# First attention of a two-block kernel: turned queries and keys kept by heads, each head's scores in four products of 32 queries

## The reference

```python
q = (layernorm(x) @ Wq).reshape(B, Sq, H, D)          # 16 batches, 128 queries, H = 16, D = 128
k = (ctx @ Wk).reshape(B, Skv, H, D)                  # 128 keys
v = (ctx @ Wv).reshape(B, Skv, H, D)
q, k = rmsnorm(q, gq), rmsnorm(k, gk)
attn = softmax(einsum('bqhd,bkhd->bhqk', q, k) / sqrt(D))
x = x + einsum('bhqk,bkhd->bqhd', attn, v).reshape(B, Sq, H * D) @ Wo
```

## Time and profile before

| | |
|---|---|
| median of 3 runs | 2107.34 us (2105.96 to 2109.98) |
| the profiled execution | 2104.1 us, its span 2102.3 us |
| mean granted TensorE clock | 0.985 |
| TensorE busy | 2030.6 us, 97% of the span |
| VectorE, ScalarE, GpSimd busy | 1341.8, 753.5, 580.9 us |
| score products (L415) busy | 142.7 us |
| send and bring | 64 of each, 512 KB, median 5.0 and 4.1 us to landing |

### The profile page before, as it was taken

One profiled execution on the slowest core, in us unless ns is written; L12 is line 12 of the kernel. 1 busy time (PEld: TensorE's weight loads), 2 busy tenths in 40 slices (PEclk: granted clock), 3 DMA queues, 4 the chain that ended last, 5 costly groups with the idle time before them and its releaser, 6 DMA issues.

```text
span 2102.3 us, 33004 instructions
## 1 busy us (share of the span) xinstructions
PE 2030.6 (97%) x12144; PEld 1665.1 (79%) x12144; DVE 1341.8 (64%) x2451; ACT 753.5 (36%) x2307; POOL 580.9 (28%) x713
## 2 busy tenths in 40 slices
PE   6999999989999889999999999999999999999999
PEld 5788888778888778888888867777778888888887
DVE  6665555565555456434335368888867888887886
ACT  4444444554444344311112145545443312222211
POOL 3322222452222232531012133333310123232321
PEclk9999999999999999999999999999999999999999
DMA  5522222333333343312002210000112256555554
GB/s 211 185 97 90 100 97 90 130 114 108 110 107 128 120 130 106 101 40 81 33 27 73 84 62 19 20 17 20 46 48 73 87 185 200 189 177 190 192 166 160
DMA packets 119503, 221.48 MB, mean 105 GB/s; under 512 B 10608, under 2 KB 65904, under 8 KB 119408
## 3 DMA queue, kind: packets, MB, share of 16 engines
q1 hardware_dynamic: 95696, 133.22, 18.8%
q0 software_dynamic: 23712, 87.04, 12.7%
HBM read 169.90 MB, written 50.33 MB: 105 GB/s over the span
## 4 chain that ended last, share of the span: by engine, by line
PE 59%; DMA 17%; DVE 11%; ACT 8%; issue 4%; POOL 1%; SPq 0%; DVEq 0%; ACTq 0%; POOLq 0%
PE bank L48 23%; PE four_banks L48 23%; DMA turned<-blocks 9%; DMA qkT<-turned 6%; PE four_banks L415 4%; ACT junk_k L514 3%; PE bank L1467 3%; ACT prob L525 3%; DVE blocks L658 2%; DVE blocks L648 2%; DVE k_sb L655 2%; PE four_banks L1538 2%; PE bank L1564 1%; PE bank L1576 1%; DVE l_rotB L1943 1%
## 5 line engine op out<-in xcount | busy, mean ns | idle before, releaser
L2363 POOL DMA_INDIRECT m_ring<-in_table,m_row x128 | 127.7, 997 | 369.6 <-DVE l_x_all L2476 263.4
L48 PE MATMUL four_banks<-l_yT_hi,m_hi 128*128 128x512 f32 x512 | 199.4, 389 | 0.0
L48 PE MATMUL four_banks<-l_yT_lo,m_hi 128*128 128x512 f32 x512 | 199.2, 389 | 0.0
L525 ACT ACTIVATE prob<-four_banks,mx,rms 128x128 f32<-128x128 f32 x256 | 113.9, 454 | 207.6 <-DVE mx L665 207.6
L415 PE MATMUL four_banks<-qkT 128*128 128x128 f32 x512 | 142.7, 436 | 31.5 <-DMA qkT<-turned 27.2
L415 PEld LDWEIGHTS four_banks<-qkT 128*128 128x128 f32 x512 | 126.6, 332 | 54.2 <-DMA qkT<-turned 53.7
L310 POOL TENSOR_TENSOR rms<-ssq,constants 128x4 f32<-128x4 f32 x128 | 26.7, 208 | 497.9 <-ACT junk_k L514 312.9
L1133 DVE TENSOR_SCALAR f_relu<-bank,f_b 128x512 f32<-128x512 f32 x64 | 48.0, 750 | 166.3 <-ACT f_h_hi L1076 166.2
L1076 ACT ACTIVATE f_h_hi<-bank,f_b 128x512 fp32r<-128x512 f32 x64 | 44.1, 690 | 256.9 <-PE bank L48 256.9
L313 POOL TENSOR_TENSOR rms<-rms,constants 128x4 f32<-128x4 f32 x128 | 130.7, 1021 | 10.0
L662 DVE TENSOR_REDUCE mx<-four_banks 128x4 f32<-128x512 f32 x64 | 44.2, 691 | 122.0 <-PE four_banks L415 122.0
(11 more groups left out here) (288 smaller groups left out, 5673.3 us busy)
## 6 DMA issues: line engine op xcount, KB each, us to landing
turned<-blocks SPq DMA_DIRECT2D x64, 512.0 KB, 5.0
qkT<-turned SPq DMA_DIRECT2D x64, 512.0 KB, 4.1
f_stage<-in_w POOLq DMA_DIRECT2D x14, 512.0 KB, 4.6
f_x_in<-x SPq DMA_DIRECT2D x18, 256.0 KB, 3.3
ctx_in<-in_ctxT SPq DMA_DIRECT2D x32, 128.0 KB, 3.5
x_in<-in_x SPq DMA_DIRECT2D x16, 256.0 KB, 2.6
x<-xres SPq DMA_DIRECT2D x16, 256.0 KB, 2.0
x<-l_x_all SPq DMA_DIRECT2D x16, 256.0 KB, 2.0
```

The source lines that it names most:

```text
L48: mm = pe.matmul(out, st, mv, start=first and n == 0, stop=last and n == len(terms) - 1)
L525: a = act.activation(prob[g][:, j, :], bank[(1, 3)[g]][:, j * P:(j + 1) * P], ACT.Exp, bias=mx[g][:, 1, j:j + 1], scale=rms[g][:, 0, j:j + 1],
L2363: pool.indirect_dma_start(ring[slot][:], None, table, bass.IndirectOffsetOnAxis(ap=row[:, tile_of(g), k:k + 1], axis=0)).then_inc(S[f"got{ ...
```

## The change

`blocks` and `qkT` are kept by slot: 32 elements of one head lie side by side, so the transposes write and the products read runs of 32 floats. A head's scores are no longer one product with 128 columns of queries held, but four with 32 each, every one into its own 32-partition strip of the bank; the keys are streamed as 4 x 32. SP issues both sends before both brings, each with a semaphore of its own. VectorE turns the queries of half 0 before it copies the probabilities of half 1. The loads, low parts and high parts of the ReLU network's weights are issued later in steps 25 to 28 (SP's behind the brings, POOL's behind the means of the queries, ScalarE's behind the squares). Two semaphores of x's pieces become one.

```diff
--- before.py
+++ after.py
@@ -115,10 +115,9 @@
     ctxp = parts("ctx", [P, KC, P])
 
 
-
     k_sb = sb("k_sb", [P, G * D], F32)
-    blocks = [sb(f"blocks{g}", [P, 4, 32, 2 * G], F32) for g in range(2)]
-    qkT = [sb(f"qkT{g}", [P, 4, 32, 2 * G], F32) for g in range(2)]
+    blocks = [sb(f"blocks{g}", [P, 4, 2 * G, 32], F32) for g in range(2)]
+    qkT = [sb(f"qkT{g}", [P, 4, 2 * G, 32], F32) for g in range(2)]
     v_sb = [sb(f"v_sb{g}", [P, G * D], F32) for g in range(2)]
     junk = {n: sb("junk_" + n, [P, slots, D], mybir.dt.bfloat16) for n, slots in (("q", G), ("k", 2 * G))}
     prob = [sb(f"prob{g}", [P, G, P], F32) for g in range(2)]
@@ -137,10 +136,10 @@
     mx = [sb(f"mx{g}", [P, 2, G], F32) for g in range(2)]
     den = [sb(f"den{g}", [P, 2, G], F32) for g in range(2)]
 
-    names = """ident_loaded x_loaded ctx_loaded xres_loaded0 xres_loaded1 xres_loaded2 xres_loaded3 xres_loaded4 xres_loaded5
-        g_loaded stats_ready ln_eps ln_ready xn_ready xT_turned xT_hi xT_lo ctx_hi ctx_split set stored eps_added qk_stored
+    names = """ident_loaded x_loaded ctx_loaded xres_loaded0 xres_loaded1 xres_loaded2 xres_loaded3 xres_loaded4
+        g_loaded stats_ready ln_eps ln_ready xn_ready xT_turned xT_hi xT_lo ctx_hi ctx_split set stored eps_added
         s_turn y_begun y_ready y_added wq0_staged wv_staged wk_staged wq1_staged wo0_staged wo1_staged""".split()
-    names += [f"{n}{g}" for g in range(2) for n in """q_made k_made v_made q_blocks k_blocks qk_loaded v_copied q_squared
+    names += [f"{n}{g}" for g in range(2) for n in """q_made k_made v_made q_blocks k_blocks qk_stored qk_loaded v_copied q_squared
         k_squared q_rms k_rms scored bias_ready exped normed p_turned pT_copied mixed oT_hi oT_lo""".split()]
     PIECES = ("wq0", "wq1", "wk0", "wk1", "wv0", "wv1", "wo0", "wo1")
     names += [f"{n}_{what}" for n in PIECES for what in ("hi", "cut")]
@@ -220,7 +219,7 @@
 
         def load_res(i):
             tiles = PIECES_OF_X[i]
-            sp.dma_start(xres[:, tiles, :], x_tiles[:, tiles, :]).then_inc(S[f"xres_loaded{i}"], 16)
+            sp.dma_start(xres[:, tiles, :], x_tiles[:, tiles, :]).then_inc(S[f"xres_loaded{min(i, 4)}"], 16)
 
         def load_x(s):
             row = sp.snap((s - NB) * P)
@@ -242,12 +241,12 @@
         def send(s, g):
             sp.wait_ge(*at(f"k_blocks{g}", s))
             sp.wait_ge(*at(f"q_blocks{g}", s))
-            sp.dma_start(turned[g].rearrange("p (j b) r -> (p j) (b r)", b=4), blocks[g][:].rearrange("p b i h -> p (b i h)")
-                         ).then_inc(S["qk_stored"], 16)
+            sp.dma_start(turned[g].rearrange("p (j b) r -> (p j) (b r)", b=4), blocks[g][:].rearrange("p b h i -> p (b h i)")
+                         ).then_inc(S[f"qk_stored{g}"], 16)
 
         def bring(s, g):
-            sp.wait_ge(S["qk_stored"], 16 * (2 * s + g + 1))
-            sp.dma_start(qkT[g][:].rearrange("d p i h -> d p (i h)"), turned[g].rearrange("p d r -> d p r")
+            sp.wait_ge(S[f"qk_stored{g}"], 16 * (s + 1))
+            sp.dma_start(qkT[g][:].rearrange("d p h i -> d p (h i)"), turned[g].rearrange("p d r -> d p r")
                          ).then_inc(S[f"qk_loaded{g}"], 16)
 
         def step(s, second_half=True, storing=True):
@@ -266,16 +265,17 @@
                 store(s - 1)
             if second_half and there(s + 3):
                 load_x(s + 3)
-            if now is not None and AHEAD_FROM <= now:
+            if now == STEPS - 2:
                 ahead["loads"](sp, now)
             if there(s + 1):
                 send(s + 1, 0)
+                send(s + 1, 1)
                 bring(s + 1, 0)
+                bring(s + 1, 1)
             if now == STEPS - 2:
                 ahead["load_x"](sp, 0, 3)
-            if there(s + 1):
-                send(s + 1, 1)
-                bring(s + 1, 1)
+            elif now is not None and AHEAD_FROM <= now:
+                ahead["loads"](sp, now)
             if now in (FIRST, 1):
                 for i, n in (((3, "wq1"),), ((4, "wo0"), (5, "wo1")))[now == 1]:
                     sp.wait_ge(S[f"{n}_cut"], 1)
@@ -345,14 +345,14 @@
             if now == NB - 1:
                 split_lo(pool, "wv0", 1)
                 split_lo(pool, "wv1", 1)
-            if now is not None and AHEAD_FROM < now < STEPS:
-                ahead["gpsimd"](pool, now)
             if there(s + 1):
                 mean(s + 1, 0, "q")
             if now == STEPS - 2:
                 ahead["root"](pool, 0, 2)
             if there(s + 1):
                 mean(s + 1, 1, "q")
+            if now is not None and AHEAD_FROM < now < STEPS:
+                ahead["gpsimd"](pool, now)
             if now == NB - 2:
                 split_lo(pool, "wq0", 1)
                 fetch("wo0", 1, after=[("wq0", 2)])
@@ -411,8 +411,9 @@
             elif there(s - 1):
                 pe.wait_ge(*at("oT_lo1", s - 1))
             for j in range(G):
-                rows = qkT[g][:].rearrange("d p i h -> d (p i) h")
-                mm = pe.matmul(bank[(1, 3)[g]][:, j * P:(j + 1) * P], rows[:, :, j], rows[:, :, G + j], start=True, stop=True)
+                for p in range(4):
+                    out = bank[(1, 3)[g]][32 * p:32 * (p + 1), j * P:(j + 1) * P].rearrange("q (p i) -> q p i", p=4)
+                    mm = pe.matmul(out, qkT[g][:, p, j, :], qkT[g][:, :, G + j, :], start=True, stop=True)
             mm.then_inc(S[f"scored{g}"], 1)
 
         def turn_p(s, g):
@@ -543,8 +544,6 @@
                 exps(s, 1)
             if now == 0:
                 split_hi(act, "wo0", 0)
-            if now is not None and AHEAD_FROM < now <= AHEAD_FROM + 4:
-                ahead["split_hi"](act, now - AHEAD_FROM - 1)
             if now == FIRST:
                 split_ctx(0)
                 split_hi(act, "wk0", 0)
@@ -577,6 +576,8 @@
                 square(s + 1, 1, "q")
             if now == NB - 2:
                 split_hi(act, "wq0", 1)
+            if now is not None and AHEAD_FROM < now <= AHEAD_FROM + 4:
+                ahead["split_hi"](act, now - AHEAD_FROM - 1)
             if now in (0, NB):
                 split_hi(act, "wo1", now // NB)
             if there(s):
@@ -614,8 +615,8 @@
 
         def statistics(s):
             if isinstance(s, int):
-                for i in {0: (0,), 1: (1,), 2: (2,), 4: (3,), 7: (4, 5)}.get(s, ()):
-                    dve.wait_ge(S[f"xres_loaded{i}"], 16)
+                for i, pieces in {0: ((0, 1),), 1: ((1, 1),), 2: ((2, 1),), 4: ((3, 1),), 7: ((4, 2),)}.get(s, ()):
+                    dve.wait_ge(S[f"xres_loaded{i}"], 16 * pieces)
             if isinstance(s, int) and s == 1:
                 dve.wait_ge(*at("xn_ready", 0))
             then(dve.bn_stats(bn[:], xres[:].rearrange("p b d -> p (b d)")[:, bass.ds(s * DM, DM)]))
@@ -645,7 +646,7 @@
 
         def turn_q(s, g):
             dve.wait_ge(*at(f"q_made{g}", s))
-            dve.transpose(blocks[g][:, :, :, 0:G].rearrange("p b i h -> p b h i"), blocks_of(bank[(7, 3)[g]][:])).then_inc(S[f"q_blocks{g}"], 1)
+            dve.transpose(blocks[g][:, :, 0:G, :], blocks_of(bank[(7, 3)[g]][:])).then_inc(S[f"q_blocks{g}"], 1)
 
         def norm_and_turn_k(s, g):
             dve.wait_ge(*at(f"k_rms{g}", s))
@@ -655,7 +656,7 @@
                 n = dve.scalar_tensor_tensor(k_sb[:, c], bank[(4, 5)[g]][:, c], rms[g][:, 0, G + j:G + j + 1], gains[:],
                                              ALU.mult, ALU.mult)
             then(n)
-            dve.transpose(blocks[g][:, :, :, G:2 * G].rearrange("p b i h -> p b h i"), blocks_of(k_sb[:])).then_inc(S[f"k_blocks{g}"], 1)
+            dve.transpose(blocks[g][:, :, G:2 * G, :], blocks_of(k_sb[:])).then_inc(S[f"k_blocks{g}"], 1)
 
         def maxima(s, g):
             dve.wait_ge(*at(f"scored{g}", s))
@@ -733,10 +734,11 @@
                 norm_and_turn_k(s + 1, 0)
             if now == FIRST:
                 split_lo(dve, "wq1", 0)
+            if there(s + 1):
+                turn_q(s + 1, 0)
             if there(s):
                 copy_pT(s, 1)
             if there(s + 1):
-                turn_q(s + 1, 0)
                 norm_and_turn_k(s + 1, 1)
             if now == FIRST:
                 split_lo(dve, "wv0", 0)
```

## The result

The changed kernel takes 2015.47 us (median of 4 runs, 2014.41 to 2016.04) against 2108.28 us for the kernel before (4 runs, 2105.96 to 2109.98): a ratio of 0.956, 95% interval 0.9543 to 0.9576. That is 93 us less, 15 more than the forecast of 2030 had it, and inside the range of 2010 to 2066. The profiled execution took 2014.41 us, its span is 2012.6 us against 2102.3.

The account below looks back on a forecast made before the run. TensorE's order was taken to bound the regular step, transport of turned queries close behind. Savings 44 + 22 + 9 + 2 = 77 us off 2104.1 gave 2027, that run being 3 under the median: 2030 us, range 2010 to 2066.

Parts of the forecast that it names:

- the last step's products: Final term of the sum: the last step's products and wait, 2 us saved.
- The score products: TensorE's scores as strips on runs of 32: 1.36 us a half instead of 2.34, 1.96 us a step saved.
- The transposes: VectorE's block transposes: 690 ns each instead of 1191 and 1135, 1.9 us less work a step before send 1.
- Send 1 and fetch 0: Transport of turned queries: send 1 takes about 2.65 us, fetch 0 lands in 4.2 to 5.0, 21.6 to 22.4 after scores.
- The regular step: Attention step without weight work: 22.2 us instead of 24.5, 2.2 us saved in each of 20, 44 us.
- The 0.15 us for mix 1: Per-step loss on TensorE because the copy of half 1's probabilities comes later behind the moved queries' transpose; 0 to 0.5.
- The long steps: Four steps of 28.4 us with weight loads: 3.2 of 3.9 us excess recovered, plus 2.2 each, 22 us.
- The seven weight steps: Steps where weights are loaded and split, partly bound by splits: 1.3 us saved each, 9 us.
- A stop at each switch of tiling: Rival: TensorE stands 0.27 us at both ends of each half's scores, losing 1.1 us a step; about 2064 us, chance 0.04.
- Strips in series: Rival: score records run one after another, 0.11 us apart, a half costing 3.94 us; 2177 us, chance 0.05.
- Fetch 0 late: Rival: fetch of half 0 lands 6 us after issue, step 23.4 us; 2061 us, chance 0.13.
- transposes unchanged: Rival: VectorE's block transposes stay at 1.15 us, step 23.9 us, saving 0.6; 2075 us, chance 0.12.

Follow-up runs that it names:

- experiment 1: Changed kernel with the loop over strips outside the loop over heads, so four products in a row share a strip: 2090.13 us, ratio 0.9939.
- experiment 6: Changed kernel with each block transpose preceded by an extra one of two of its heads, lengthening VectorE's work: 2067.01 us, ratio 0.9817.
- experiment 9: Changed kernel with ScalarE's, POOL's and SP's parts of the next stage's weights in steps 25 to 28 back in their old places: 2021.15 us, ratio 0.9602.
- experiment 10: Kernel before with only POOL's and ScalarE's parts of the weights of steps 25 to 28 in their new places: 2089.1 us, ratio 0.9925.
- experiment 2: Kernel before with four score products of 32 queries a head in strips, on the old layout: 2096.99 us, ratio 0.9973.
- experiment 11: Changed kernel with the queries' transpose of half 0 back behind the copy of half 1's probabilities: 2016.91 us, ratio 0.9582.
- experiment 12: Changed kernel with step 14's 1 MB weight load moved behind the means of the queries: 2004.68 us, ratio 0.9535.
- experiment 3: Kernel before with the new layout and score products, but old order of sends, queries' transpose and weights: 2035.48 us, ratio 0.9678.
- experiment 7: Changed kernel with the old layout and old score products, keeping the new order and later weights: 2112.79 us, ratio 1.0041.
- experiment 4: Changed kernel with the old order send 0, fetch 0, send 1, fetch 1: 2024.79 us, ratio 0.963.

## Why the prediction was right, step by step

The mechanism was the one forecast, and the forecast of 2030 us was 15 us too slow. The sum was made for the profiled execution: 77 us forecast off, 90 measured (2104.1 - 2014.41). Timelines, kernel before and after: start of the first and the last step's scores 0.

```profile
33.67 1.09 PE L415 MATMUL four_banks<-qkT 128*128 128x128 f32 x4
...
830.82 2.16 PE L415 MATMUL four_banks<-qkT 128*128 128x128 f32 x8
```

```profile
33.80 1.40 PE L416 MATMUL four_banks<-qkT 128*32 128x128 f32 x32 [1.91 <-DMA qkT<-turned]
...
740.72 1.08 PE L416 MATMUL four_banks<-qkT 128*32 128x128 f32 x32
```

The 31 steps are 797.15 - 706.92 = 90.2 us shorter, as is the span (89.7): nothing is gained or lost behind the last scores 0. So the 2 us that the sum had for the last step's products did not come; they are too small to trace, since the stretch from there to the end lies between 1267.6 and 1274.1 us in the kept traces (1271.5 before, 1271.9 after).

- **The score products**: 1.36 us a half forecast, 1.35 measured. L1564 was the right row to price them by, and experiment 1 shows that its order of strips is part of the price. The reading "a quarter of 0.11" was luck in part: the records in one strip need 0.071, not 0.11, and the overlap is 2.7 times and not 4.
- **The transposes**: 690 ns forecast, 712 and 675 measured. That they lie on the way to send 1 and count nearly whole is shown by experiment 6.
- **Send 1 and fetch 0**: the forecast had send 1 leave 16.95 us after the scores' start; the second send is issued just before 211.28, some 17.1 after 193.89. Fetch 0 takes the lower of my two ends, 4.2 to 4.3 us, and is there some 0.3 us before TensorE.
- **The regular step**: 22.2 forecast, 22.06 measured, 2.45 us saved and not 2.2: 49 us instead of 44. I had placed the step between TensorE's 22.0 and the transport's 21.6 to 22.4; it is TensorE's alone. The 0.15 us for mix 1 did not come; holes of 0.08 and 0.09 us before the scores came in its place.
- **The long steps**: 3.2 of the 3.9 us given back was the forecast, all of it came: 113.61 - 88.24 = 25 us instead of 22. Experiments 9 and 10 show the cause, but also that it is not additive: the weights' places are worth 15 us in the kernel before and 9 to 10 in the changed one (6 of them in the trace's four steps), where the sends go out first.
- **The seven weight steps**: this term was mis-sized most, 9 us forecast, 90.2 - 49 - 25.4 = 16 measured. I took them for partly bound by the weights' splits, at 1.3 us each. Half of it is at the change of weights (112.50 us from 383.54 to 496.04 before, 104.68 after), the rest is shared by the start and one step at 160, whose send 0 took 4.55 us in the kernel before and which is now a regular 22.06. Why that send was slow, with no other transfer of size in flight, stays open.
- **A stop at each switch of tiling** was a rival. At the size that it was given, 1.1 us a step on top of the forecast, it is excluded: a half costs 1.35 us and the forecast was 1.36. But the prediction's "no stop is seen" at L1564 was a wrong reading, since every product here starts before the modelled end of the one ahead of it. The 0.21 us that it found there, and put into the sum, is much longer than the 0.03 between records. So the trace does not speak against the rule that the prediction sets beside that row. Rows of full-width products show that this gap, and the small hole ahead, come with the strips. Kernel before, a mix, and scores of a half that had no wait:

```profile
320.32 1.05 PE L429 MATMUL four_banks<-pT_sb,v_sb 128*128 128x128 f32 x8
321.13 0.48 PE L48 MATMUL bank<-wq_hi,xT_hi 128*128 128x512 f32 x1
...
701.18 0.40 PE L48 MATMUL four_banks<-wo_hi,oT_lo 128*128 128x512 f32 x1
701.42 2.04 PE L415 MATMUL four_banks<-qkT 128*128 128x128 f32 x8
```

  The full-width scores, behind the same semaphores, start 0.24 us after the product ahead of them, that is with no hole, while the scores in strips start at least 0.31 after it, in the changed kernel and in experiment 2. Behind the last record of L429 (at 320.32 + 1.05 - 0.27 = 321.10) the next product follows in 0.03 us, behind the last strip record in 0.20. So 0.08 to 0.09 us ahead and 0.17 behind belong to the strips, about 17 us in 64 halves. That it is the switch of tiling, and nothing else about the strips, is not shown. From the start of the records to the next product the full-width L429 takes 0.81 us and the strips take 1.01. An estimate from these rows: full-width products on operands in runs would make a half 0.3 us cheaper than the strips do. No run tried them.
- **Strips in series** was the rival on the slower side. Its price was wrong: at the 0.071 us a record of experiment 1 a half would cost 31 x 0.071 + 0.53 = 2.73 us, and the regular step of the kernel so ordered is in fact longer than before, 24.82 us against 24.5. That kernel is still 0.6% faster than the one before, and not by the scores: of the 14 us that its 31 steps are shorter, the four long steps give 14 (24.8 us each instead of 28.4) and the weight steps 6, and the regular steps take 6 back. The rival's 2177 us failed on its pace of 0.11.
- **Fetch 0 late, transposes unchanged**: excluded by the rows above. The first came true only where a big load falls among the sends (experiments 11 and 12), and by 0.9 us a step with the longer transposes of experiment 6.

How the 93 us divide depends on the order in which one counts. Layout and products alone give 3.2% (experiment 3). The new order with the weights' places costs 0.4% alone (experiment 7) and gives 1.2% on top of the layout: with slow transposes the fetch of half 0, held until send 1 is out, becomes the limit, and with fast ones it does not. The weights' places by themselves give 0.75% of it in the kernel before (experiment 10), the order of sends by itself 0.7% in the changed one (experiment 4). Nor can the layout's gain be shared out between the two engines. The reads of the scores save 64 x 0.98 = 63 us of TensorE, and experiment 1, which adds 88 us to TensorE, makes the kernel 80 us slower; without the short transposes 56 us are lost (experiment 6). Together that is more than 93: each needs the other. Short transposes with the old reads were not run.

## What to carry to other kernels

Look at the steps of the innermost index on both sides of a layout: here one choice of order in a buffer made TensorE read and VectorE write at about half pace, and mending the reads with transposes as slow as before keeps 37 of the 93 us (experiment 6). Before an order of DMAs is changed, count how late its producer is; issuing both sends before both fetches gained 0.7% with a fast producer (experiment 4) and, together with the queries' transpose moved ahead, lost 1.2% with a slow one (experiments 7 and 10). Keep large loads that have time off the microseconds around a transfer on the loop's path, and find out which engine really sets their time: it was not the one that issues them.

## What the runs showed of the hardware that I had not expected

- fp32 records of 32 held columns and 128 streamed start 0.071 us apart in one strip and 0.026 with neighbours in different strips, a factor of 2.7 and not 4; a record with 128 held columns needs 0.11.
- With elements 32 bytes apart the same records start 0.058 apart over four strips, 2.2 times as slow as in runs of 32 floats, the same factor as for full-width products (0.24 to 0.11).
- A block transpose of 512 elements takes 675 to 712 ns when it writes in runs and 1120 to 1200 with a step of 32 bytes, from PSUM and from SBUF alike.
- 128x32 records among full-width products cost about 0.26 us a burst beyond their own pace: a hole of 0.08 to 0.09 us ahead, where full-width scores have none, and 0.20 us from the last record to the next product, where L429 has 0.03.
- In a regular step a 512 KB send takes 2.6 to 2.9 us when no fetch is in flight and 5.0 when a fetch was issued 0.5 us ahead of it. The fetch beside it takes 4.2 us whether it is issued about 0.5 us ahead of the send (before) or behind it (after).
- A 1 MB load among the sends made send 1 take 6.2 us and fetch 0 7.2 in the changed kernel; the scores waited 2.9 us there, and 6.0 in experiment 11, where the load follows send 0 more closely.
